# A routed feed-forward stage cut into 36 slots instead of 39, with half slots shared by two experts and the split expert weights ranked and reloaded

## The reference

```python
xn = rms_norm(x, norm_scale)
scores = jnp.einsum('bsd,ed->bse', xn, w_router)
_, ids = jax.lax.top_k(scores, 2)
c = jnp.take_along_axis(jax.nn.softmax(scores, axis=-1), ids, axis=-1)
val, gate = jnp.split(jnp.einsum('bsd,ehd->bseh', xn, w_up), 2, axis=-1)   # H = 704
y = jnp.einsum('bseh,edh->bsed', val * jax.nn.silu(gate), w_down)
out = jnp.sum(jnp.take_along_axis(y, ids[..., None], axis=2) * c[..., None], axis=2) + x
```

## Time and profile before

| | |
|---|---|
| median of 3 runs | 421.23 us (420.44 to 421.67) |
| the profiled execution | 421.26 us |
| its span, first to last instruction | 419.4 us |
| mean granted TensorE clock | 0.971 of full |
| TensorE busy | 375.3 us (89%) |
| VectorE, ScalarE, GpSimd busy | 265.6, 242.4, 180.3 us |

### The profile page before, as it was taken

One profiled execution on the slowest core, in us unless ns is written; L12 is line 12 of the kernel. 1 busy time (PEld: TensorE's weight loads), 2 busy tenths in 40 slices (PEclk: granted clock), 3 DMA queues, 4 the chain that ended last, 5 costly groups with the idle time before them and its releaser, 6 DMA issues.

```text
span 419.4 us, 9669 instructions
## 1 busy us (share of the span) xinstructions
PE 375.3 (89%) x2491; PEld 268.6 (64%) x2492; DVE 265.6 (63%) x672; ACT 242.4 (58%) x451; POOL 180.3 (43%) x184
## 2 busy tenths in 40 slices
PE   5699999999998066999899999999999999999981
PEld 5578888888886042566466666666666666666650
DVE  2799678898886986877766664454445445445440
ACT  3499965877765386778556544545444444454440
POOL 2545545765556002346345444334434434433321
PEclk9899999999999659999999999999999999999998
DMA  7999873452225602143243343334334343333411
GB/s 226 404 423 409 317 242 113 135 167 76 76 83 195 193 1 64 28 65 63 53 76 57 57 77 58 68 65 68 58 63 71 55 74 65 55 72 63 63 16 24
DMA packets 45302, 47.57 MB, mean 113 GB/s; under 512 B 25696, under 2 KB 41056, under 8 KB 44128
## 3 DMA queue, kind: packets, MB, share of 16 engines
q1 hardware_dynamic: 37200, 36.28, 26.8%
q0 software_dynamic: 7536, 10.52, 15.9%
q10 hardware_dynamic: 544, 0.52, 0.4%
HBM read 32.83 MB, written 9.50 MB: 101 GB/s over the span
## 4 chain that ended last, share of the span: by engine, by line
PE 71%; ACT 8%; DVE 8%; issue 5%; DMA 4%; POOL 1%; POOLq 0%; SPq 0%; DVEq 0%; ACTq 0%
PE bank L1339 32%; PE bank L1366 5%; PE bank L1390 5%; PE bank L1391 5%; PE bank L1392 5%; ACT arena L464 3%; PE bank L1200 3%; PE bank L1254 3%; PE bank L1263 2%; ACT arena L479 2%; DMA arena<-in_w 2%; PE bank L1142 1%; PE bank L1151 1%; PE bank L1160 1%; PE bank L1158 1%
## 5 line engine op out<-in xcount | busy, mean ns | idle before, releaser
L1339 PE MATMUL bank<-expert_w,arena 128*128 x702 | 152.0, 362 | 3.9 <-issue 1.1
L772 POOL DMA_INDIRECT out<-arena,add_idx x39 | 67.5, 1732 | 128.1 <-ACT arena L646 128.1
L1339 PEld LDWEIGHTS bank<-expert_w,arena 128*128 128x128 f16 x702 | 66.9, 98 | 65.1 <-issue 12.1
L761 POOL DMA_INDIRECT arena<-xrow_hbm,take_idx x39 | 40.0, 1026 | 42.8 <-DVE add_idx L1055 22.6
L1116 DVE SCALAR_TENSOR_TENSOR arena<-bank,dn_small,arena 128x512 f32<-128x512 f32 x78 | 45.3, 580 | 18.5 <-PE bank L1339 15.9
L1103 DVE COPY arena<-bank 128x1024 f16<-128x1024 f16 x39 | 26.9, 690 | 44.0 <-PE bank L1366 44.0
L668 ACT ACTIVATE arena<-arena 128x512 f16<-128x512 f32 x39 | 24.5, 629 | 51.7 <-DVE arena L1116 51.7
L1390 PE MATMUL bank<-expert_w,arena 128*128 x195 | 53.2, 273 | 1.0 <-DVE arena L1103 0.9
L1391 PE MATMUL bank<-expert_w,arena 128*128 x195 | 53.2, 273 | 0.0
L1392 PE MATMUL bank<-expert_w,arena 128*128 x195 | 53.2, 273 | 0.0
L1122 DVE TENSOR_TENSOR arena<-arena 128x512 f16<-128x512 f32 x39 | 27.0, 693 | 28.4 <-ACT arena L668 28.4
(11 more groups left out here) (191 smaller groups left out, 679.4 us busy)
## 6 DMA issues: line engine op xcount, KB each, us to landing
expert_w<-in_wup SPq DMA_DIRECT2D x8, 1408.0 KB, 18.0
expert_w<-in_wdn SPq DMA_DIRECT2D x8, 640.0 KB, 4.7
rows<-in_x SPq DMA_DIRECT2D x8, 256.0 KB, 7.5
arena<-in_ctxT SPq DMA_DIRECT2D x8, 256.0 KB, 3.2
xrow_hbm<-front SPq DMA_DIRECT2D x8, 256.0 KB, 2.3
out<-rows SPq DMA_DIRECT2D x8, 256.0 KB, 2.7
rows<-in_wup SPq DMA_DIRECT2D x1, 1408.0 KB, 6.0
expert_w<-in_wdn SPq DMA_DIRECT2D x16, 64.0 KB, 4.5
```

The lines of the kernel that those rows point to most:

```text
L761: pool.indirect_dma_start(out=xs_row[:, i % 2], out_offset=None, in_=xrow_hbm, in_offset=bass.IndirectOffsetOnAxis(ap=take_idx[:, i:i + 1] ...
L772: pool.indirect_dma_start(out=out, in_=yt[:, i % 2], in_offset=None, out_offset=bass.IndirectOffsetOnAxis(ap=add_idx[:, i:i + 1], axis=0), ...
L1339: last = T.matmul(bank[q][:, 0:n], xsT[:, slot, 2 * a + c], up_w[:, ds(w0 + c * UPC + w * 2 * H + lo, n)], start=m == 0, stop=m == len(pro ...
```

## The change

1. **Slots.** The rows of an expert are counted in halves of 64. Whole slots are filled first, and the remaining halves of two experts share a "mixed" slot: 32 whole (`UNIFORM`) and 4 mixed (`MIXED`), 36 in all. In a mixed slot every matmul of the up and the down product is issued twice with 64 stationary columns, once for PSUM partitions 0 to 63 and once for 64 to 127, each with its expert's weights. The order is 28 whole slots, then mixed and whole in turn. A mixed slot is added to the output in two DMAs, the second after the first has landed.
2. **Weights.** Experts are ranked by their number of whole slots. The buffer has nine regions; rank 0's weights are split from the raw weights there, and for ranks 1 to 7 SyncE reloads the raw weights from HBM, an up load (1408 KB) after the transpose of an odd slot and a down load (640 KB) after an even one. All 32 halves of up and down are split in stage E, steps 1 to 22, by ScalarE and VectorE. Stage A squares one up half a step, stage B the other up halves and the down weights, and splits nothing. For the mixed slots SyncE copies the second expert's split weights inside SBUF to a fixed place.
3. **Stage E's order.** All engines' steps are written out, with no hardware loop. The down product of a slot stands two slots behind its up product instead of one, with two buffers for transposed `h` and two PSUM banks for `y`; the transposes of `h` come after all three up parts.
4. **Routing.** 34 links until a pair's column instead of 25, five more behind the columns, and the slots' experts from a small matmul (`place`) that follows the slot table; the probabilities are divided on GpSimd. The stored rows of `xn` have two buffers.

Core of the diff:

```diff
-        NSLOT = 2 * NT + NE - 1
+        UNIFORM, MIXED = 2 * NT, NE // 2
+        NSLOT = UNIFORM + MIXED
-        MARK_LINKS, TILE_LINKS = 14, 27
-        COL_LINKS, DVE_COLS = 25, 2 * NT - 8
+        MARK_LINKS, COL_LINKS, TILE_LINKS, TABLE_LINKS = 13, 34, 35, 48
+        DVE_COLS = 2 * NT - 7
+        ORDER = list(range(UNIFORM - MIXED)) + [n for q in range(MIXED) for n in (UNIFORM + q, UNIFORM - MIXED + q)]
+        FIRST_SLOT = [0, 4, 7, 11, 14, 18, 21, 25]
+        SPLIT_STEPS = range(1, 3 * NE - 1)
+        HALF_UP_AFTER, HALF_DOWN_AFTER = (23, 25, 30, 32), (24, 26, 33, 35)
 # SyncE
             for i in range(1, NSLOT):
                 sp.wait_ge(s_xs[i % 2], 16 * (i // 2) + 16)
                 if i >= 2:
                     sp.wait_ge(s_up, 3 * i - 3)
                 sp.dma_start_transpose(xsT[:, i % 2], xs[:, i % 2, 0:4 * P]).then_inc(s_xsT[i % 2], 16)
+                if i <= 2 * (NE - 1):
+                    if i % 2:
+                        fetch_up((i + 1) // 2)
+                    else:
+                        fetch_down(i // 2)
+                for q in range(MIXED):
+                    if HALF_UP_AFTER[q] == i:
+                        copy_half_up(q)
...
 # GpSimd
             for i in range(NSLOT):
                 pool.wait_ge(s_yt, i + 1)
-                if i:
-                    pool.wait_ge(s_add, 16 * i)
-                pool.indirect_dma_start(out=out, in_=yt[:, i % 2], ...add_idx[:, i:i + 1]...)
+                for m in range(2 if mixed(i) else 1):
+                    if i or m:
+                        pool.wait_ge(s_add, added(i) + 16 * m)
+                    pool.indirect_dma_start(out=out, in_=yt[:, i % 2], ...rows_of...)
                 if i + 4 < NSLOT:
                     take(i + 4)
 # TensorE, step_e; i = r - 1
+                    pe.wait_ge(s_xsT[i % 2], 16 * (i // 2) + 16)
+                    up(i, home[i], 0, 0, HA, lows)
+                    up(i, home[i], 1, HA, HA, ...)
+                    up(i, home[i], 2, 2 * HA, 2 * HB)
                 if live(r, 2, NSLOT):
+                    ... transposes of h of slot i - 1
+                if live(r, 3, NSLOT):
+                    j = i - 2
+                    if j >= 2:
+                        pe.wait_ge(s_yt, j - 1)
+                    down(j, home[j])
 # TensorE, one matmul of up(i)
+                    if mixed(i):
+                        T.matmul(bank[q][0:half, 0:n], x[:, 0:half], split_w[:, ds(home + (c * UPC + at_w), n)], **flags)
+                        last = T.matmul(bank[q][half:P, 0:n], x[:, half:P], half_up[...][c][:, at_w:at_w + n], **flags)
 # ScalarE, step_e: y is scaled at the end of the step, no longer ahead of silu
+                    act.wait_ge(s_y, j + 1)
+                    nc.scalar.activation(yt[:, j % 2], bank[6 + j % 2][:, 0:D], ACT.Copy, scale=pair_scale[:, j:j + 1]).then_inc(s_yt, 1)
```

More of the change, by code:

```diff
@@ L618, in _ @@
             act.wait_ge(s_rtr, NBATCH)
+            for slot in range(2):
+                act.wait_ge(s_row[slot], 16 * NBATCH // 2)
             for n in range(DVE_COLS, 2 * NT):
@@ L1192, in _ @@
             pe.wait_ge(s_uT, NBATCH)
-            pe.wait_ge(s_sq, 2 * NE)
-            T.matmul(bank[1][:, 0:2 * NE], const("ones"), sq, start=True, stop=True).then_inc(s_fro, 1)
             def keys(slot):
@@ L1318, in _ @@
             last.then_inc(s_tab, 1)
-            keep_clock(3)
+            keep_clock(2)
+            pe.wait_ge(s_rd, TABLE_LINKS)
+            T.matmul(bank[6][:, 0:2 * TAB], const("ones"), place, start=True, stop=True).then_inc(s_place, 1)
+            keep_clock(1)
             pe.wait_ge(s_xs[0], 16)
@@ L1336, in up, with load_home @@
+            half = P // 2
+            def load_home(i):
+                return pe.snap(pe.value_load(slot_home[0:1, ORDER[i]:ORDER[i] + 1], min_val=0, max_val=(NE - 1) * 2 * EXP))
+            def up(i, home, q, lo, n, lows=None, between=None):
                 for m, (c, a, w) in enumerate(products):
-                    if m == 3 and between:
+                    if m == 2 and between:
                         between()
-                    last = T.matmul(bank[q][:, 0:n], xsT[:, slot, 2 * a + c],
-                                    up_w[:, ds(w0 + c * UPC + w * 2 * H + lo, n)],
-                                    start=m == 0, stop=m == len(products) - 1)
@@ L1342, in up @@
-                last.then_inc(s_up, 1)
+                    if w and not c and lows:
+                        pe.wait_ge(s_lo, lows)
+                    flags = dict(start=m == 0, stop=m == len(products) - 1)
+                    x = xsT[:, i % 2, 2 * a + c]
+                    at_w = w * 2 * H + lo
+                    if mixed(i):
+                        T.matmul(bank[q][0:half, 0:n], x[:, 0:half], split_w[:, ds(home + (c * UPC + at_w), n)], **flags)
+                        last = T.matmul(bank[q][half:P, 0:n], x[:, half:P], half_up[(ORDER[i] - UNIFORM) % 2][c][:, at_w:at_w + n], **flags)
+                    else:
+                        last = T.matmul(bank[q][:, 0:n], x, split_w[:, ds(home + (c * UPC + at_w), n)], **flags)
@@ new lines, in up, with down @@
+                last.then_inc(s_up, 1)
+            def down(j, home):
+                y = bank[6 + j % 2][:, 0:D]
+                pairs = [(c, c, w) for c in range(NH - 1) for w in range(2)]
+                pairs += [(NH if c == NH - 2 else NH + 1 + c, c, 0) for c in range(NH - 1)] + [(NH - 1, NH - 1, 0), (NH - 1, NH - 1, 1)]
+                pairs.sort(key=lambda v: v[1])
+                for m, (block, c, w) in enumerate(pairs):
+                    flags = dict(start=m == 0, stop=m == len(pairs) - 1)
+                    h = hT[j % 2][:, block]
+                    if mixed(j):
+                        at_w = dn_at(c, w) - 2 * UPC
+                        T.matmul(y[0:half], h[:, 0:half], split_w[:, ds(home + dn_at(c, w), D)], **flags)
+                        last = T.matmul(y[half:P], h[:, half:P], half_dn[(ORDER[j] - UNIFORM) % 2][:, at_w:at_w + D], **flags)
+                    else:
+                        last = T.matmul(y, h, split_w[:, ds(home + dn_at(c, w), D)], **flags)
+                last.then_inc(s_y, 1)
```

797 lines of the change are left out of this document (419 added, 378 removed).

## The result

The changed kernel takes 487.57 us (485.59 to 489.78, 4 runs) against 420.84 (420.42 to 421.67) for the kernel before on the same chip: a ratio of 1.157, 95% interval 1.153 to 1.162. I had forecast 448 with a range to 468. The direction was right, the size was not: 67 us were lost where I had 27. Medians and ranges here are over all runs of a kernel; the ratios leave out runs that were over 1.5% above the fastest of their kernel.

What follows compares the result with a forecast made beforehand. TensorE was taken to bound the kernel before; afterwards the exposed gather path would bind. The steps summed to 440.0 us, plus 4 for reloads and 2 for scaling: 446, forecast 448, own range 437 to 459, with rivals 435 to 468.

Steps and rivals of the forecast that it cites:

- The sum: Whole kernel: first up product at 162.0, stage E's steps and closing adds, 440.0 us in the profiled execution's own span.
- C: Stage E: path from finished `y` through scaling, add, gather and transpose to transposed rows, 8.0 us.
- W: Stage E: TensorE's work in one step, 6.05 us for a whole slot, 6.8 for a mixed one.
- The mechanism: Stage E: gather behind the add binds; TensorE waits about 2 us, two steps take 14.05 us.
- Reloads, 4 us: Stage E: 14 loads slow gather and transpose, 4 us, bounds 0 to 18; rival at full 18 us, chance 0.08.
- mostly over by the next gather: Stage E: a load issued behind a transpose hardly overlaps the following gather; the reason for taking 4 us.
- Late scaling, 2 us: Stage E: ScalarE's second down half precedes scaling `y` in one step of three, 7 steps, about 2 us.
- Slots 28 to 35: Late stage E: mixed up product 6.4 us; steps 31 and 33 wait for mixed adds, 19.05 us each.
- Mixed halves: Mixed slots in stage E: the two 64-column halves run side by side, W = 6.8 us a slot.
- rival of one after the other: Mixed slots: halves run in sequence, 11.4 us work a slot, 465 us in all; chance 0.20.
- The adds at the end: Kernel's end: four adds in line at 4.25 us spacing, the last issued at 431.75; 7 us cost.
- Stages A, B and routing: Before stage E: stages A and B together -1.5 us (-3 to +1), routing +2.4 (+1 to +5).

Runs made afterwards that it cites:

- no reloads: The changed kernel without the 14 weight reloads and the two waits for them, so splits read wrong weights: 479.55 us (476.93 to 483.62).
- no reloads, filler: Changed kernel without reloads and their waits, plus three fp32 matmuls of 384 columns before the transposed rows' wait in odd steps from 5: 472.26 us.

## Why the prediction was right in kind and wrong in size

The step that failed is the price of the wait. The sum takes the path of the rows at its quiet landings (C = 8.0 us), leaves the step behind the wait at W = 6.05 us with no term for TensorE's clock, and gives the reloads 4 us. All three were too small; what follows says what each measured. The table sets the sum against three kernels, from the starts of the up products (us):

```
                     sum    changed   no reloads   no reloads, filler
first up product    162.0    159.7      161.7        161.1
slots 0 to 3         14.2     19.3       15.2         15.2
slots 3 to 23       140.5    171.6      160.1        153.6
slots 23 to 28       36.1     42.6       42.3         42.3
slots 28 to 35       59.3     63.9       67.3         66.7
behind slot 35       27.9     30.5       30.7         30.6
span                440.0    487.6      477.3        469.4
```

- **The mechanism**: right. Waits in every second step up to slot 17, ended by the transpose; gather ahead of the add removes nearly all of them (7.5 us are left between 160 and 340) and 67 us. TensorE is not the bound.
- **The path C, 8.0 us**: mis-sized. From the up product of an odd slot to the next one it measured 8.3 to 9.3 us without reloads (mean 8.75 of seven, slots 5 to 18) and 8.4 to 11.7 with them (mean 10.2 of the seven up to slot 16, the first included). Add and gather were issued as forecast (0.90, 1.90), and the transpose cost 2.4 to 2.5; it was the gather, at 2.8 in the rows, that landed in 3.4 (no reloads) and 4.7 (with). The first wait, behind slot 3, was 10.2 to 10.3 in the three kernels of the table; without reloads GpSimd took 2.87 us instead of 1.59 to issue its add.
- **W of the waiting step, 6.05 us**: mis-sized by the clock, which the sum leaves out. It fell after idles of 2.1 to 4.1 us without reloads, in six of seven waiting steps of slots 4 to 16, 1.5 to 1.7 us each, 9.9 together; the filler got 6.5 us back in slots 3 to 23, and the whole kernel was 7.3 faster. This is a cost that grows out of the wait.
- **Slots 3 to 23 without reloads, added up**: 19.6 us over the sum, of which 7.5 are the path in eight waits, 9.9 the clock, and 2.2 slots 18 to 23.
- **Reloads, 4 us** (bounds 0 to 18): mis-sized. 11.5 us in slots 3 to 23 and 4 in slots 0 to 3, where a transpose stood behind the first one; 8 of these were left at the end. Inside the bounds, so by itself this would have given 452 to 460. The sentence "mostly over by the next gather" failed: a load of 1,408 KB took 5.9 us to land, not 3.4, and the gather beside it 4.7. The rule of turns between queues that I cited (the Trainium skill, "DMA: Bandwidth & Descriptors", SWDGE vs HWDGE vs iDMA) is borne out in so far as no gather stood behind a whole load: the slowest landed in 6.0 us, where 2.8 and a whole load would be 8.7. The slowing was not small for it.
- **Late scaling, 2 us**: hardly seen. Without reloads the add behind the waiting step was issued 0.95 us after the up product's start in five cases of seven and 1.06 in two.
- **Copies of half weights, priced at nothing**: slots 23 to 28 took 6.5 us more than the sum. By an estimate from the pace of the kernel without reloads (8.0 a slot in slots 3 to 23), 4 of these are the same path and clock and about 2 the copies'. No run takes the copies out.
- **Slots 28 to 35**: 4.6 us over the sum. The two pairs with two adds ahead of a gather took 20.0 and 19.2 us where the sum has 19.05 each, so that term was right; the rest is in the pair before them (16.8 for 14.4) and the last step (8.0 for 6.8).
- **Mixed halves**: right, side by side. The rival of one after the other falls.
- **The adds at the end**: right in spacing, two short in number, 2.6 us.
- **Stages A, B and routing**: 2.3 us better than the sum in this execution; other runs with the same stages A and B started at 158.8 to 161.7.

The errors of C, W and the reloads all had one sign and were all in one place, the wait. My range took the bounds of each term one at a time. The path and the clock of slots 3 to 23 without any reload (17.4 us) lift 448 less the 4 for the reloads to 461, above my own range of 437 to 459. From slot 23 on that kernel took another 17 us more than the sum.

Open: why a gather takes 3.4 us instead of 2.8 with no reload beside it. It isn't the low clock (3.6 with the filler); the work of splitting the weights, which ScalarE and VectorE do in the same slots, was in all these runs and is not ruled out. Nor did a run tell whether it is the volume of the reloads or how many transfers stand at once that stretches the adds.

## What to carry to other kernels

When one product moves a stage later in a pipeline, walk through every engine's list for what waits for its result and what stands behind that wait: here a gather that needed nothing of it cost 67 us by standing behind it, and moving one call cured it. Once a transfer is on the path, price it by how it lands among the transfers of that stretch and add what the clock does in the product behind each idle; both enter in every period, so small errors multiply. Adds to the output that wait for one another are a resource with a rate (4.0 to 5.4 us from one to the next here): count them per step as one counts an engine's time.

## What the hardware showed that I had not expected

- Behind idles of 2.1 to 4.1 us a product of 18 matmuls took 5.1 to 5.4 us instead of 3.74, the first part of it at the lower of the clock's two levels (1.2 and 2.4 GHz; granted clock 0.51 in that part, 0.84 to 0.91 in long windows with such steps). Behind 4.4 to 5.5 us it took 5.4 to 6.6. The length of the idle alone does not decide: 2.90 us once left it at 3.74, and 2.10 us once did not.
- With the large loads in ScalarE's queue the transposes in SyncE's landed in 6.9 us (median of those with a landing time), and the kernel took 7 us more than with all of them in one queue.
- A load of 1,408 KB took 5.9 us to land beside other traffic, where 421 GB/s, the rate of stage A, would make it 3.4. Windows with a DMA share of 0.87 moved only 233 GB/s (the kernel with the gather first).
- Two fp16 matmuls with 64 stationary columns each and different output partitions cost together what one with 128 costs: 0.22 us for 512 columns.
